# Values per head or values shared by all heads in a decoder's cross-attention

## What is computed

```python
q = x @ Wq                      # [1024, 16 heads, 64]
k = context @ Wk                # [6404, 16, 64]
v = context @ Wv                # [6404, 16, 64]
p = softmax(q @ k.T / sqrt(64)) # per head
y = (p @ v) @ Wo + bo           # = (p @ context) @ (Wv @ Wo), per head
```

## Time and profile before

| | us |
|---|---|
| median of three runs | 4694.61 (4685.64 to 4712.13) |
| profiled execution, device time | 4716.16 |
| its span, first to last instruction | 4714.4 |
| plain chunks, first `tf` to last | 123.7 to 929.2 |
| the other 28 chunks | 929.2 to 3302 |
| tail, tiles | 3400.4 to 4471.8 |

### The profile page before, as it was taken

One profiled execution on the slowest core, in us unless ns is written; L12 is line 12 of the kernel. 1 busy time (PEld: TensorE's weight loads), 2 busy tenths in 40 slices (PEclk: granted clock), 3 DMA queues, 4 the chain that ended last, 5 costly groups with the idle time before them and its releaser, 6 DMA issues. The chain is left out here.

```text
span 4714.4 us, 105294 instructions
## 1 busy us (share of the span) xinstructions
PE 3969.0 (84%) x38240; PEld 2143.3 (45%) x38240; DVE 3658.0 (78%) x15825; ACT 2850.1 (60%) x9049; POOL 1046.6 (22%) x1207
## 2 busy tenths in 40 slices
PE   4767777648999999999999999999588988898759
PEld 2333343334545445445454454544255555555436
DVE  4787888778888888887888888886678888887541
ACT  2555555535666666666666666667177777777712
POOL 1000000000000000000000000000288878888700
PEclk7555555557999999999999999999599999999969
DMA  2222222100000000000000000000312221222020
GB/s 62 66 70 70 68 70 70 60 3 3 2 4 4 2 4 2 3 4 2 3 2 3 3 2 3 2 2 3 93 39 71 73 73 42 67 72 58 3 57 5
DMA packets 97822, 146.85 MB, mean 31 GB/s; under 512 B 14077, under 2 KB 90549, under 8 KB 92150
## 3 DMA queue, kind: packets, MB, share of 16 engines
q1 hardware_dynamic: 97302, 140.13, 10.7%
HBM read 82.32 MB, written 56.56 MB: 29 GB/s over the span
## 5 line engine op out<-in xcount | busy, mean ns | idle before, releaser
L1270 PEld LDWEIGHTS G<-st,rec_w 128*128 128x128 f16 x19456 | 609.9, 100 | 894.7 <-DVE st L1430 854.6
L1664 POOL TENSOR_TENSOR plt<-pft,pht 128x512 f16<-128x512 f32 x765 | 875.2, 1169 | 244.2 <-DVE pht L1891 163.8
L1270 PE MATMUL G<-st,rec_w 128*128 128x1 f16 x19456 | 684.3, 165 | 286.9 <-DVE st L1430 268.8
L1222 PE MATMUL OA<-pf,vals 128*97 128x512 f32 (+1 forms) x1632 | 855.3, 605 | 0.7
L1166 ACT ACTIVATE st<-hb 32x16 f16<-32x16 f32 x1216 | 259.0, 213 | 704.0 <-DVE hb L1425 703.3
L267 DVE TENSOR_REDUCE mx<-MT 128x1 f32<-128x512 f32 (+1 forms) x832 | 520.9, 661 | 96.0 <-PE MT L1710 92.2
L1659 ACT ACTIVATE pft<-ST,ln_prob 128x512 f32<-128x512 f32 (+1 forms) x816 | 541.0, 687 | 64.1 <-PE ST L1732 63.5
L267 DVE TENSOR_REDUCE mx<-MB 128x1 f32<-128x512 f32 (+1 forms) x832 | 537.4, 660 | 48.2 <-PE MB L259 33.5
L1146 ACT ACTIVATE pf<-SC,ln_prob 128x512 f32<-128x512 f32 (+1 forms) x816 | 560.7, 687 | 20.5
L1657 ACT ACTIVATE pht<-ST,ln_prob 128x512 f16<-128x512 f32 x510 | 350.9, 688 | 264.4 <-PE ST L1732 259.0
L1157 ACT ACTIVATE tf<-G 32x16 f32<-32x16 f32 x1216 | 213.0, 175 | 366.3 <-PE G L1270 338.0
(11 more groups left out here) (321 smaller groups left out, 7484.2 us busy)
## 6 DMA issues: line engine op xcount, KB each, us to landing
vc<-scr_v SPq DMA_DIRECT2D x16, 1644.8 KB, 15.9
kc<-scr_k SPq DMA_DIRECT2D x32, 816.0 KB, 13.1
scr_v<-v_hl SPq DMA_DIRECT2D x24, 1032.0 KB, 5.6
scr_k<-k_hl SPq DMA_DIRECT2D x192, 128.0 KB, 1.7
k<-scr_k SPq DMA_DIRECT2D x16, 816.0 KB, 6.7
w<-in_L_ffn_W SPq DMA_DIRECT2D x16, 256.0 KB, 5.8
xin<-x SPq DMA_DIRECT2D x38, 48.0 KB, 1.8
scr_v<-v_hl SPq DMA_DIRECT2D x2, 774.0 KB, 5.7
```

The costliest lines, as they stand in the source:

```text
L1222: pe.matmul(OA[0:at.DC + 1, :], at.vals[0:rows, i, :], pf[0:rows, tile % 2, :], start=(i == 0), stop=(i == KT - 1)).then_inc(pv_done, 1)
L1270: mm = pe.matmul(g[:, t, c:c + 1], rec_w[:, c, :], st[:, c:c + 1], start=False, stop=(c == C - 1), skip_group_check=True)
L1664: return eng.tensor_tensor(pl[0:k, t % NP_, :], pf[0:k, t % NP_, :], ph[0:k, t % NP_, :], ALU.subtract)
```

## The change

The plain chunks make only the keys. `KeysByHead` gives its 104 products eleven places of a chunk. The values are no longer made per head: the setup makes `vals_c`, the scaled context in f16 as 96 high values, a one and 96 low values, which stays in SBUF for all heads. The tail uses it in place of `vc`, so the high matmuls stream 193 columns and the low ones 97; the loads of `vc` and the wait for them go. Sums, transposes and the projection have 96 instead of 64 values a row, and the projection uses `vo_w` (the product of the two weights, which the middle stage uses already) in place of `wo_t`.

```diff
@@ Attention
-        self.wo_t = sb("wo_t", [DHEAD, HEADS, D])
+        self.vals_c = sb("vals_c", [P, KT, 2 * DC + 1], F16)
+        self.vo_w = sb("vo_w", [DC, HEADS, D])
...
-        self.wv_h = sb_inside("wv_h", [DC, HEADS * DHEAD], F16)
-        self.wv_l = sb_inside("wv_l", [DC, HEADS * DHEAD], F16)
-        self.vo_w = sb_inside("vo_w", [DC, HEADS, D])
@@ attention_prepare
+                pool.memset(at.vals_c[:, :, DC:DC + 1], 1.0)
...
-                s.activation(at.wk_h[:, :], wk_sb[:, :], ACT.Copy)
-                s.activation(at.wv_h[:, :], wv_sb[:, :], ACT.Copy).then_inc(w_hi, 1)
-                s.activation(at.wo_t[:, :, :], wo_sb[:, :, :], ACT.Copy, scale=1.0 / at.C_SCALE)
+                s.activation(at.wk_h[:, :], wk_sb[:, :], ACT.Copy).then_inc(w_hi, 1)
                 a.wait_ge(d_ctx, 32)
                 s.activation(at.vals[:, :, 0:DC], ctx_f[:, :, :], ACT.Copy, scale=at.C_SCALE)
+                s.activation(at.vals_c[:, :, 0:DC], ctx_f[:, :, :], ACT.Copy, scale=at.C_SCALE).then_inc(v_hi, 1)
...
-                v.tensor_tensor(at.wv_l[:, :], wv_sb[:, :], at.wv_h[:, :], ALU.subtract)
+                dve.wait_ge(v_hi, 1)
+                dve.wait_ge(d_ctx, 32)
+                v.scalar_tensor_tensor(out=at.vals_c[:, :, DC + 1:], in0=ctx_f[:, :, :], scalar=at.C_SCALE,
+                                       in1=at.vals_c[:, :, 0:DC], op0=ALU.mult, op1=ALU.subtract)
@@ the places
-    PLACES = (0, 1, 2, 3, 4, 5, 7, 8, 11, 12, 13, 14, 15, 18, 19, 20, 21, 25, 28, 30, 31)
+    PLACES = (0, 2, 4, 7, 8, 11, 12, 15, 18, 19, 21)
@@ slstm_stage, chunks: the value branches go on SP, ACT, PE and DVE; the key branches stay as they were
-        v_hl = sb("v_hl", [P, 2, at.HEADS // 2, ByHead.TILES_A_STORE, 2 * at.DHEAD + 1], F16)
...
-                    pool.memset(v_hl[:, :, :, :, at.DHEAD:at.DHEAD + 1], 1.0)
...
-                        elif by_head.values[i - by_head.n_keys][3]:
...
-                            sp.dma_start(values_out[heads, :, j0:j + 1, :].rearrange("h p t c -> p h t c"),
-                                         v_hl[:, b, :, 0:j + 1 - j0, :]).then_inc(d_vals[b], 16)
...
-                                    pe.matmul(out, at.keys_l[:, rows], at.wv_h[:, cols], start=True, stop=False)
-                                    pe.matmul(out, at.keys_h[0:at.DC, rows], at.wv_l[:, cols], start=False, stop=False)
-                                    pe.matmul(out, at.keys_h[0:at.DC, rows], at.wv_h[:, cols], start=False,
-                                              stop=True).then_inc(k_full, 1)
...
-                                    s.activation(hi, product, ACT.Copy).then_inc(k_hi, 1)
...
-                                    v.tensor_tensor(low, product, hi, ALU.subtract).then_inc(k_low, 1)
@@ attention_tail
-    VC = 2 * DHEAD + 1
+    VC = 2 * DC + 1
...
-        vc = sb("vc", [P, 2, KT, VC], F16)
...
-                load_values(0)
...
-                    sp.wait_ge(pv_done, KT * (g + 1))
-                    load_values(g + 2)
...
-                            mm = pe.transpose(XP[0:DHEAD, i * P:(i + 1) * P], o_n[:, i, :], at.identa[:, :])
+                            mm = pe.transpose(XP[0:DC, i * P:(i + 1) * P], o_n[:, i, :], at.identa[:, :])
...
-                            mm = pe.matmul(XP[:, i * P:(i + 1) * P], o_t[:, i * P:(i + 1) * P], at.wo_t[:, g - 1, :],
+                            mm = pe.matmul(XP[:, i * P:(i + 1) * P], o_t[:, i * P:(i + 1) * P], at.vo_w[:, g - 1, :],
...
-                    if j == 0:
-                        pe.wait_ge(d_vc[g % 2], 16 * (g // 2 + 1))
...
-                                  vc[0:k, g % 2, j, :], start=(j == 0 and i % 2 == 0), stop=False, skip_group_check=True)
+                                  at.vals_c[0:k, j, :], start=(j == 0 and i % 2 == 0), stop=False, skip_group_check=True)
...
-                        mm = pe.matmul(OA[i // 2][:, (i % 2) * 256:(i % 2) * 256 + DHEAD + 1], pl[0:k, t % NP_, i * P:(i + 1) * P],
-                                       vc[0:k, g % 2, j, 0:DHEAD + 1], start=False, stop=(j == KT - 1), skip_group_check=True)
+                        mm = pe.matmul(OA[i // 2][:, (i % 2) * 256:(i % 2) * 256 + DC + 1], pl[0:k, t % NP_, i * P:(i + 1) * P],
+                                       at.vals_c[0:k, j, 0:DC + 1], start=False, stop=(j == KT - 1), skip_group_check=True)
...
-                        v.tensor_copy(o_low[:, 2 * c:2 * c + 2, :], pair[:, :, DHEAD:VC]).then_inc(o_lo, 1)
+                        v.tensor_copy(o_low[:, 2 * c:2 * c + 2, :], pair[:, :, DC:VC]).then_inc(o_lo, 1)
```

More of the change, by code:

```diff
@@ L427, in __init__, with item, before_store, after_store @@
         assert len(self.load) == len(self.store) == len(ends)
-class ByHead:
-    PLACES = (0, 1, 2, 3, 4, 5, 7, 8, 11, 12, 13, 14, 15, 18, 19, 20, 21, 25, 28, 30, 31)
+class KeysByHead:
+    PLACES = (0, 2, 4, 7, 8, 11, 12, 15, 18, 19, 21)
     T_STORE = 18
-    TILES_A_STORE = 4
     def __init__(self, at, chunks, chunk_steps):
[L438 to L442, removed]
-        self.n_keys, self.total = len(self.keys), len(self.keys) + len(self.values)
-        self.v_stores = 2 * -(-at.KT // self.TILES_A_STORE)
-        places = [c * chunk_steps + p for c in range(chunks) for p in self.PLACES]
-        assert self.total <= len(places)
-        self.at_step = {s: i for i, s in enumerate(places[:self.total])}
-    def in_chunk(self, chunk, late):
-        return [i for s, i in self.at_step.items()
-                if s // self.chunk_steps == chunk and (s % self.chunk_steps >= self.T_STORE) == late]
-def slstm_stage(nc, x, w, scratch_in, scratch_out, dims, at, first_row, xa_out, keys_out, values_out):
+        self.pieces = [(c * 512, min(c * 512 + 512, at.KT * P)) for c in range(-(-at.KT * P // 512))]
+        total = at.HEADS // 2 * len(self.pieces)
+        places = [c * chunk_steps + p for c in range(chunks) for p in self.PLACES]
+        assert total <= len(places)
+        self.at_step = {s: i for i, s in enumerate(places[:total])}
+        self.total = total
+    def item(self, i):
+        pair, c = divmod(i, len(self.pieces))
+        return pair, *self.pieces[c]
+    def before_store(self, chunk, chunk_steps):
+        return [i for s, i in self.at_step.items() if s // chunk_steps == chunk and s % chunk_steps < self.T_STORE]
+    def after_store(self, chunk, chunk_steps):
+        return [i for s, i in self.at_step.items() if s // chunk_steps == chunk and s % chunk_steps >= self.T_STORE]
+def slstm_stage(nc, x, w, scratch_in, scratch_out, dims, at, first_row, xa_out, keys_out):
     S, D, L, H, K, UP = dims
@@ L768, in slstm_stage @@
         d_keys = [sem(f"d_keys{i}") for i in range(2)]
-        d_vals = [sem(f"d_vals{i}") for i in range(2)]
-        def value_parts(by_head, i):
-            group, half, j, _ = by_head.values[i - by_head.n_keys]
-            store, slot = 2 * group + half, j % by_head.TILES_A_STORE
-            b = store % 2
-            return (store, b, v_hl[:, b, :, slot, 0:at.DHEAD], v_hl[:, b, :, slot, at.DHEAD + 1:],
-                    SC[i % 2][:, :].rearrange("p (h d) -> p h d", d=at.DHEAD))
         def bc(ap, n):
@@ L1054, in _ @@
                         if by_head:
-                            for i in by_head.in_chunk(p, True):
-                                store(i)
+                            for i in by_head.after_store(p, CH):
+                                store_keys(i)
                         if plan and p in plan.load:
@@ L1551, in attention_tail @@
         pl = sb("plt", [P, NP_, N], F16)
-        o_low = sb("o_low", [P, NB, DHEAD + 1])
-        o_n = sb("o_n", [P, NB, DHEAD])
-        o_t = sb("o_t", [DHEAD, N])
+        o_low = sb("o_low", [P, NB, DC + 1])
+        o_n = sb("o_n", [P, NB, DC])
+        o_t = sb("o_t", [DC, N])
         y_all = sb("y_all", [P, TILES, D])
@@ L1792, in _ @@
                 for i in range(NB):
-                    mm = pe.matmul(XP[:, i * P:(i + 1) * P], o_t[:, i * P:(i + 1) * P], at.wo_t[:, HEADS - 1, :],
+                    mm = pe.matmul(XP[:, i * P:(i + 1) * P], o_t[:, i * P:(i + 1) * P], at.vo_w[:, HEADS - 1, :],
                                    start=True, stop=True)
@@ L1844, in keep_sums @@
                         dve.wait_ge(o_lo, 2 * g + c + 1)
-                        v.tensor_tensor(o_n[:, 2 * c:2 * c + 2, :], pair[:, :, 0:DHEAD], o_low[:, 2 * c:2 * c + 2, 1:DHEAD + 1],
+                        v.tensor_tensor(o_n[:, 2 * c:2 * c + 2, :], pair[:, :, 0:DC], o_low[:, 2 * c:2 * c + 2, 1:DC + 1],
                                         ALU.add).then_inc(o_free, 1)
```

89 lines of the change are left out of this document (32 added, 57 removed).

## The result

| | before | after |
|---|---|---|
| median of 20 runs each | 4696.88 (4685.64 to 4712.37) | 4683.59 (4667.0 to 4696.59) |
| ratio after / before | | 0.9966, 95% interval 0.9954 to 0.9979 |
| profiled execution, device time | 4716.16 | 4678.55 |
| its span | 4714.4 | 4676.8 |
| setup, to the first `tf` | 123.7 | 126.7 |

The plain chunks came out as worked out; the tail grew by 13 us in this pair of profiles, far less than the 57 of the sum.

What follows compares the result with a forecast made beforehand. Bound: a chain of small operations in plain chunks; in the tail no full engine, but a three-tile VectorE-TensorE loop. Terms -41.8 + 4.2 + 53 + 4 = +20 us on 4694.6 gave 4715 us; range 4673 to 4763.

Steps and rivals of the forecast that it cites:

- Plain chunks: Ten chunks: value products go, key products spread from 21 to 11 places; 76.3 us a chunk, -41.8 us together.
- The two sorts of cost: Plain chunks: products waiting for an earlier product's low part and store; and the VectorE subtraction lying ahead of `uu`.
- Setup: Before the first `tf`: VectorE's subtraction over 4896 elements replaces one of 1024, in series; +4.2 us.
- Price of the columns: Tail matmuls: 0.42 ns a column, 0.16 us more a tile, 131 us of added TensorE work for 16 heads.
- How much lands: Tail: of the 131 us added, 3.3 us a head lengthens the time, +53 us; ends 20 and 131.
- the three-tile loop: Tail: VectorE reductions and TensorE maxima wait for each other over three tiles, about 3.9 us; a third of added work lands.
- The four sums of a head: Tail, VectorE: two `o_low` copies and two `o_n` sums a head grow 0.07 us each; +4 us.
- C: Rival: tail hides the columns almost to the limit; 20 to 35 us land, 4681 to 4697 us; chance 0.13.
- D: Rival: longer matmuls bring fewer half-clock stretches in the tail, about 18 us back; 4673 us or less; chance 0.10.
- B: Rival: TensorE becomes the tail's bound; +87 to +131 us land, 4749 to 4793 us; chance 0.20.
- E: Rival: plain chunks give only half, 24 us instead of 42; 4733 us; chance 0.05.
- Signs in the profile: Full-clock head in the tail: 69 us, or 67.5 for C; TensorE idle 7 to some 3 us; longer GpSimd cast waits.

Runs made afterwards that it cites:

- e5: Kernel after with the 104 key products put back at the old 21 places of a chunk; 4700.8 us, ratio 1.0007.
- e9: Kernel before with VectorE's casts of `pht` written as a maximum over groups of one element; 4653.5 us, ratio 0.9889.
- e10: Kernel after with VectorE's casts of `pht` written as a maximum over groups of one element; 4657.9 us, ratio 0.9894.
- e4: Kernel after with the tail's value matmuls at the old 129 and 65 columns in all but each head's first tile; 4669.4 us, ratio 0.9930.
- r1: Second profile of the kernel after, unchanged; 4677.8 us, tail 1092.3 us.
- e3: Kernel after with the tail's low matmuls streaming all 193 columns instead of 97; 4755.5 us, ratio 1.0107.
- e2: Kernel before with ScalarE making every `pht` and VectorE casting none; 4610.7 us, ratio 0.9800.
- e7: Kernel after with ScalarE making every `pht`, plus a VectorE reduction of a spare tile after waiting for `pft` in 6 of 16 tiles; 4673.9 us, ratio 0.9943.

## Why the prediction was wrong

- *Plain chunks, -41.8.* Right: 763.0 us against 805.5, -42.5. The two sorts of cost were read rightly; e5 shows the share of the places. That the chunk came out at 76.3 to the tenth is partly luck: in the mean of chunks 1 to 8 the steps behind places 11 and 12 are 0.34 and 0.36 us longer than in the bare chunk, as worked out, but the one behind place 19 is 0.09 longer, not 0.24, and steps 0, 2 and 4 add 0.26, which the working left out, while step 25 is 0.19 shorter.
- *Setup, +4.2.* Right in kind: +3.0 in the first pair, +3.2 by the means of three profiles of after and two of before.
- *Price of the columns, 131 us of TensorE's work.* Right.
- *How much lands, 53.* This step failed: 20 landed, which is the least that the prediction's own count of free time allowed, and the tail grew by 23 at equal clock (13 in the first pair) where the sum had 57. With it the sum turns from +20 to -16.5. "So of three tiles of TensorE one is on the chain" was read from one stretch of the timeline, where TensorE and VectorE's reductions wait for each other. Those waits are there, but they are smaller (77.9 us of TensorE's loads for `mx` in the tail of before) beside the 241 us that TensorE waited for `plt`; I named that item in passing ("besides the loads' wait for GpSimd") and did not follow it to its end: `plt` waits for the cast, and the cast is held until `plt`'s engine is done. As e9 and e10 show, this exclusion set the pace, and TensorE's idle time beside it took the columns in. The note that the prediction is wrong "if the three-tile loop is not what sets the tail's pace" was the case. A cast of 0.9 us in the median against a least of 0.41 stood in the trace of before.
- *The four sums of a head, +4.* The work is as priced: `o_low` takes 0.355 us against 0.288, `o_n` 0.347 against 0.280. How much of it lands is not shown: e4, which keeps it, is about 3 us above before at the same clock, but it also keeps the wide columns in the first tile of each head, 2.6 us of work.
- *The sum.* The terms add up to +19.4, written as +20, and the rivals' times are up to 1 us off in the same way; nothing hangs on it.
- *Rivals.* C (it hides almost to the limit) gave 4681 to 4697 and holds the result; its reason, though, was spare room by the count, with no word on what sets the pace. D (fewer stretches at half clock) looked right in the first pair and falls with r1 and with the mean clocks of all executions. B (TensorE becomes the bound of the tail) is the state that e3 came near. E (the plain chunks give half) falls with the 763.0 us.
- *Signs in the profile.* A head at full clock went from 65.7 to 67.3 us in the median, where I had named 67.5 as the mark of C and 69 as that of the forecast; 16 times 1.6 us is 26, near the 23 at equal clock. TensorE's idle time per head fell from 7 to 3 us, and GpSimd's waits for the cast grew from 163.8 to 186.9 us, both as named, so neither sign could tell the forecast from what happened.

## What to carry to other kernels

Before a share of added work is charged to the path, take the longest wait of the engine that gets the work and follow it, releaser by releaser, until an engine waits for nothing. If that ends elsewhere, the work is cheap as long as the engine has idle time (118 us here, not the 241 of the listed wait), and dear from there on. The price also changes when the pace-setter is removed: 23 us here with the exclusion, 63 without it. Compare the least and the median duration of one instruction form: where they differ by a factor of two, the instruction may wait inside itself, and no list of waits shows it. Where VectorE's casts and GpSimd's operations both work on SBUF, try the conversions on ScalarE or in a form that leaves GpSimd alone; here that gave 92 and 46 us (e2, e9).

## What the runs showed of the hardware

- A VectorE cast from SBUF to SBUF (128x512, f32 to f16) takes 0.41 us alone. Begun under a GpSimd operation that reads SBUF, it ends 0.28 us after that operation.
- The same conversion as a reduction over one element takes 0.68 us and is not held up. The Trainium skill (SBUF — State Buffer, Who interferes with whom) says that a reduction never contends on this chip; e7, e9 and e10 agree.
- A GpSimd memset of one row of 13056 f16 elements took 10.97 us, with 128x128 normalisations on VectorE held up for all of it.
- Time at half clock in the tail changed from 24 to 54 us between executions of one kernel, in which 30 us more cost 12.6.
